# Maxima last in the transposed scores, and the query, key and transposed-score products next to each other

## What is computed

```
win    = windows of x, 64 tokens each               # (8*16, 64, 128)
normed = layernorm(win) * ln1_g + ln1_b
q,k,v  = split(normed @ in_w.T + in_b), 8 heads of 16
attn   = softmax(q @ k.T / 4)                       # 64 x 64 for each window and head
y      = win + (attn @ v) @ out_w.T + out_b
y      = y + silu(layernorm2(y) @ fc1_w.T + fc1_b) @ fc2_w.T + fc2_b
```

## Time and profile before

| | |
|---|---|
| median of three runs | 374.71 us (373.15 to 374.91) |
| profiled execution | 375.25 us, its span 373.4 us |
| PE matmul busy | 346.6 us, 93% |
| DVE, ACT, POOL busy | 293.6, 241.8, 167.2 us |
| one image in the loop | about 41.9 us: 23.0 us for the odd step (158.94 to 181.99) and 18.9 us for the even step (181.99 to 200.87), from scores 0 to scores 0 |
| granted TensorE clock | 0.986 of full speed on average |

### The profile page before, as it was taken

The page is one execution under the profiler, slowest core; times in us unless marked ns, Lnnn a source line. Parts: engine busy times, 40 slices in busy tenths (PEclk is TensorE's granted clock), DMA queues, the critical chain, the costliest instruction groups (busy, mean ns, idle before and its releaser), DMA issues.

```text
span 373.4 us, 9822 instructions
## 1 busy us (share of the span) xinstructions
PE 346.6 (93%) x3349; PEld 292.5 (78%) x3349; DVE 293.6 (79%) x862; ACT 241.8 (65%) x438; POOL 167.2 (45%) x176
## 2 busy tenths in 40 slices
PE   3678999999999999999999999999999999999764
PEld 2477788888888888888888888888888888878552
DVE  8478889798798878798798878798798878686552
ACT  1425678684968578684968578684969578665440
POOL 6353064636446434635456434635455434441420
PEclk9989999999999999999999999999999999999898
DMA  4132130302122121303122121303122120300001
GB/s 130 31 92 71 43 87 31 88 27 65 64 83 71 30 82 56 94 19 76 59 75 70 34 78 56 101 11 77 63 72 68 35 77 31 87 2 28 30 1 56
DMA packets 31715, 21.98 MB, mean 59 GB/s; under 512 B 22417, under 2 KB 23505, under 8 KB 31697
## 3 DMA queue, kind: packets, MB, share of 16 engines
q1 hardware_dynamic: 31696, 21.75, 21.3%
HBM read 4.95 MB, written 4.19 MB: 24 GB/s over the span
## 4 chain that ended last, share of the span: by engine, by line
PE 75%; DVE 6%; issue 5%; ACT 2%; POOL 1%; DVEq 0%; POOLq 0%; ACTq 0%
PE p_scoreT L635 12%; PE p_c L530 12%; PE p_score L612 9%; PE p_attn L650 9%; PE p_a L530 6%; PE p_scoreT L630 4%; PE p_a L594 4%; PE p_c L708 4%; PE p_d L530 3%; DVE xn_tok L1106 3%; PE p_c L679 2%; PE p_a L578 2%; PE p_a L568 2%; PE p_c L685 2%; PE p_c L666 1%
## 5 line engine op out<-in xcount | busy, mean ns | idle before, releaser
L912 ACT ACTIVATE probs<-p_scoreT 128x512 f32<-128x512 f32 x64 | 38.6, 603 | 34.6 <-PE p_scoreT L635 34.1
L466 POOL TENSOR_TENSOR hid_l<-hid,hid_h 128x512 fp32r<-128x512 f32 x30 | 40.4, 1365 | 43.0 <-ACT hid_h L946 41.2
L612 PE MATMUL p_score<-kd_h,qd_h 128*128 128x128 f32 (+1 forms) x512 | 54.7, 250 | 0.8 <-DVE row_max L1159 0.8
L612 PEld LDWEIGHTS p_score<-kd_h,qd_h 128*128 128x128 f32 (+1 forms) x512 | 50.4, 164 | 5.8 <-DVE row_max L1159 2.2
L650 PEld LDWEIGHTS p_attn<-vd,probs 128*64 128x64 f32 x1024 | 36.2, 139 | 22.2 <-issue 15.1
L471 POOL TENSOR_TENSOR y_l<-y,y_h 128x512 fp32r<-128x512 f32 (+1 forms) x17 | 20.6, 1210 | 70.3 <-ACT y_h L926 70.3
L1159 DVE TENSOR_REDUCE row_max<-p_score 128x8 f32<-128x512 f32 x64 | 43.9, 686 | 7.9 <-PE p_score L612 7.9
L650 PE MATMUL p_attn<-vd,probs 128*64 128x34 f32 x1024 | 45.6, 245 | 2.6 <-ACT probs L912 2.6
L635 PE MATMUL p_scoreT<-qd_h,kd_h 128*128 128x256 f32 x128 | 41.6, 325 | 0.0
L458 POOL TENSOR_SCALAR kd_l<-k_l,head_a 128x512 fp32r<-128x512 f32 x16 | 26.7, 1670 | 32.2 <-DVE k_l L1141 21.1
L450 POOL TENSOR_TENSOR rstd<-rstd,minus_half 128x4 f32<-128x4 f32 (+1 forms) x33 | 35.5, 1075 | 2.8
(11 more groups left out here) (182 smaller groups left out, 871.0 us busy)
## 6 DMA issues: line engine op xcount, KB each, us to landing
x_in<-in_x SPq DMA_DIRECT2D x16, 256.0 KB, 2.8
qd_h<-q_h SPq DMA_DIRECT2D x64, 64.0 KB, 2.0
qd_l<-q_l SPq DMA_DIRECT2D x64, 64.0 KB, 2.0
vd<-v_tok SPq DMA_DIRECT2D x64, 64.0 KB, 2.2
out<-out_sb SPq DMA_DIRECT2D x16, 256.0 KB, 2.1
fc_rows<-in_L_conv_fc_w SPq DMA_DIRECT2D x2, 128.0 KB, 2.5
in_w_rows<-in_L_conv_in_w SPq DMA_DIRECT2D x1, 192.0 KB, 2.7
out_w_rows<-in_L_conv_out_w SPq DMA_DIRECT2D x1, 64.0 KB, 2.5
```

The source lines that it names most:

```text
L466: pool.tensor_tensor(hid_l[:, t], hid[:, t], hid_h[:, t].bitcast(F32), ALU.subtract).then_inc(hid_low[t], 1)
L612: last = pe.matmul(p_score[0:rows, 2 * KEYS * j:2 * KEYS * (j + 1)], qd_h[:, h.par, j, 2 * KEYS * p:2 * KEYS * p + rows], kd_h[:, h.par, 2 ...
L912: act.activation(probs[:, p % 2], p_scoreT[:].rearrange("row (win j q) -> row win j q", win=2, j=QUADS), ACT.Exp, scale=SCORE_SCALE).then_ ...
```

## The change

Two things are changed. In `b_scoreT`, the six products come first and the four maxima products last; the wait for `max_wide_ready` stands between them, and for p = 0 three waits (for the spread queries and keys) are repeated ahead of the products. In the steps, PE does `c_kv` ahead of `a_q`, and `a_k` directly behind `a_q` and ahead of `b_scoreT(b, 1)`; before, `a_k` stood behind `b_score(b, 3)` and `d_kvT`. ACT's list moves its own `a_k` ahead of the exponential of p = 1 accordingly. DVE's, POOL's and SP's lists are unchanged.

```
             def b_scoreT(h, p):
 
-                pe.wait_ge(max_wide_ready[p], h.n())
                 if p == 0:
+                    pe.wait_ge(q_high_dma, h.n(times=16 * QUADS))
+                    pe.wait_ge(kd_high[0], h.n())
+                    pe.wait_ge(kd_high[1], h.n())
                     pe.wait_ge(q_low_dma, h.n(times=16 * QUADS))
...
                 dst = p_scoreT[:].rearrange("row (win j q) -> row win j q", win=2, j=QUADS)
-                for j in range(QUADS):
-                    pe.matmul(dst[:, :, j, :], max_wide[:, p % 2, 2 * j:2 * j + 2, :],
-                              neg_ident[:], start=j == 0, stop=False, skip_group_check=True)
                 for win in range(2):
                     window = 2 * p + win
                     for k, (kd, qd) in enumerate(((kd_h, qd_h), (kd_h, qd_l), (kd_l, qd_h))):
-                        last = pe.matmul(dst[:, win], kd[:, h.par, window], qd[:, h.par, :, KEYS * window:KEYS * (window + 1)],
-                                         start=False, stop=win == 1 and k == 2, skip_group_check=True)
+                        pe.matmul(dst[:, win], kd[:, h.par, window], qd[:, h.par, :, KEYS * window:KEYS * (window + 1)],
+                                  start=win == 0 and k == 0, stop=False, skip_group_check=True)
+                pe.wait_ge(max_wide_ready[p], h.n())
+                for j in range(QUADS):
+                    last = pe.matmul(dst[:, :, j, :], max_wide[:, p % 2, 2 * j:2 * j + 2, :],
+                                     neg_ident[:], start=False, stop=j == QUADS - 1, skip_group_check=True)
                 last.then_inc(scoreT_ready[p], 1)
...
                 b_attn(b, 0)
                 if with_c:
                     c_yT(c)
-                if with_a:
-                    a_q(a)
                 if with_tail:
                     c_kv(tail)
+                if with_a:
+                    a_q(a)
+                    a_k(a)
                 b_scoreT(b, 1)
                 b_score(b, 3)
                 if with_d:
                     d_kvT(loop, -1)
-                if with_a:
-                    a_k(a)
                 b_attn(b, 1)
...
                 if with_a:
                     a_q(a)
+                    a_k(a)
                 b_exp(b, 1)
                 if with_a:
-                    a_k(a)
                     a_k_block(a, 0)
```

More of the change, by code:

```diff
@@ L779, in step @@
                     c_yT(c)
+                if with_tail:
+                    c_kv(tail)
                 if with_a:
                     a_q(a)
-                if with_tail:
-                    c_kv(tail)
+                    a_k(a)
                 b_scoreT(b, 1)
```

## The result

The changed kernel takes 372.49 us in the median of ten runs (370.96 to 377.03), against 375.12 us (373.09 to 376.27) for the kernel before on the same chip: ratio 0.9924, with an interval of 0.9901 to 0.9946. The forecast was 373.2 us, range 371.0 to 376.0. So it is faster, by 0.8% where 0.4% was forecast. Three of the ten, near 377.0 us, ran at a lower granted clock (0.966 or 0.967 on average, the others 0.984 to 0.990), and the ratio leaves them out.

The account below looks back on a forecast made before the run. PE's list, busy 93% of the span, was taken as the bound. Odd steps -1.9, even steps +0.9, last odd step -0.35 and image 1's even-step wait -0.15 gave -1.5 us: 373.2 us against the median, range 371.0 to 376.0.

Parts of the forecast that it names:

- odd, scores 1 to projection with its bare load: PE at the start of odd steps: the wait for `max_wide` goes, 1.96 to 1.79 us, 0.17 gained.
- odd, `c_yT` to attention 1: PE in odd steps: key products beside the query products shorten this stretch from 5.33 to 5.07 us, 0.26 less.
- odd, p = 2 in front of `d_mT`: Odd steps, where `d_mT` follows the scores of p = 2: maxima last loses 0.04 us (0 to 0.08).
- odd, `d_final` late by DVE: Odd steps: `d_final` waits for DVE's second-block matrix, which may come late; 0.08 us lost, between 0 and 0.3.
- even, scores 1 to projection: PE in even steps: 1.74 to 1.79 us, 0.05 lost, about half hidden where attention 0 waits for ACT.
- even, attention 1 waits for the exponential: Even steps: attention 1 directly follows scores 3 and waits for ACT's exponential, 4.57 to 4.63 us, 0.06 lost.
- even, `xn_tok` later: DVE's statistics chain in even steps comes 0 to 0.70 us later, delaying PE's next odd step; 0.05 us taken.
- The price of 0.08: On PE, each full load of 128 fp32r columns behind a short bf16 product leaves 0.08 us not hidden.
- part 1 alone gives zero: Maxima last in `b_scoreT`: by the bare loads alone nothing is gained, one of 0.08 us leaves and one comes.
- the slower rival: Even steps, `row_max` of p = 3 to `xn_tok`: DVE's delay passed on whole, +4.6 us, to 377.8 us; chance 0.12.
- the whole gain arrives: Rival: no give-backs, odd steps -0.43 us, even steps 0, in all -3.1 us, to 371.6 us; chance 0.26.
- The bound does not move: Rival: odd steps' gain is spent waiting for ACT or DVE, -0.2 us a loop image or less, 374.3 us; chance 0.18.

Follow-up runs that it names:

- part1: Kernel before with the maxima products last in all four transposed scores, the old order of the steps kept: 374.63 us, ratio 0.9995.
- extra_full2: Changed kernel plus one unused DVE reduction of 0.68 us in every even step, ahead of the statistics: ratio 0.9990 to the kernel before.
- last01: Changed kernel with the maxima last only at p = 0 and 1, first again at p = 2 and 3: 371.59 us, ratio 0.9917 to the kernel before.
- aggregate2: Changed kernel with DVE aggregating the next half's statistics ahead of `yn_l` in even steps: ratio 0.9926 to the kernel before.
- norm_early: best2 with DVE doing `yn_tok` ahead of `row_max` of p = 3 in even steps: ratio 0.9948 to the kernel before.
- best2: aggregate2 with the maxima last only at p = 1 and, in odd steps, p = 0: ratio 0.9941 to the kernel before.

## Why the prediction was right, and where its sizes were off

The direction and the mechanism held, but the sum for an image of the loop was half of what came. The profile's span lost 2.9 us where -1.5 was forecast; the fourteen steps of the middle lost 2.07 where the sum has -1.9 + 0.9 - 0.15 = -1.15. The forecast's steps, before to after, in means over the loop:

| step of the forecast | forecast | measured |
|---|---|---|
| odd, scores 1 to projection with its bare load | 1.96 to 1.79 | 1.95 to 1.79 |
| odd, `c_yT` to attention 1 | 5.33 to 5.07 | 5.33 to 5.05 |
| odd, p = 2 in front of `d_mT` | +0.04 | +0.06 |
| odd, `d_final` late by DVE | +0.08 | 0.00 |
| odd, p = 3 | 0 | +0.01 |
| even, scores 1 to projection | +0.05, half hidden | +0.05, of which 0.02 comes back by `c_yT` |
| even, attention 1 waits for the exponential | 4.57 to 4.63 | 4.57 to 4.59 |
| even, `xn_tok` later | +0.05 | about +0.01 |
| even, p = 2 | 0 | -0.02 |
| even, p = 3 | 0 | +0.11 |
| odd, wait at `a_back` | 0 | -0.10 |

- **The price of 0.08 was right**, and so were both sums made from it. The projection's group grew from 0.70 to 0.78 and scores 3 in odd steps from 0.73 to 0.82. The first score product took 0.12 behind the key products and 0.17 behind the scores. The three repeated waits cost nothing that shows: scores 1 take the 0.74 of the sum. In the trace of the change a load of 128 fp32 columns takes 188 ns in the median (L634) and one of 128 bf16 columns 98 ns (L638). By the Trainium skill ("TensorE: Matmul & The Clock Gate", section "LDWEIGHTS (loading the stationary operand)") a load of 128 columns, at 107 ns, would leave some 0.05 bare (0.06 by its figure), an estimate; the trace doesn't agree, since the rows at the new places say 0.08 again and the fp32 loads last longer, so the measurement decides. That part 1 alone gives zero held: part1 changed an image by 0.01.
- **Mis-sized, `d_final`.** I took 0.08 a step in odd steps. The first `d_final` group stands at the same distances before and after (2.20 behind `d_mT`). DVE's matrix was not the last to arrive.
- **Mis-sized, the exponential.** Forecast +0.06, measured +0.02 to 0.03. The wait exists, 0.06 in the rows above, but the exponential starts 3.94 behind `c_yT`, where my sum had 3.71 + 0.22 + 0.05 = 3.98.
- **Mis-sized, and the larger error, the end of the even step.** I called the trade at p = 2 and 3 even except in front of `d_mT`. In the even step's p = 3 it isn't: behind the attention, whose loads have 64 columns, the first L634 now takes 0.22 (last rows of the even step above), and a second bare load stands behind the maxima in front of `fc1`. That is +0.11 (2.50 to 2.61), which the sum had left out. But it costs nothing: from the even step's transposition to `a_back` of the next step PE took 5.85 us before and 5.86 after. This stretch ends with PE's wait for `xn_tok`, so PE's 0.11 there only eats that wait (scores 0 to `a_back` 1.09 to 0.99). I had priced PE's wait as something that could only grow.
- **A term with no row in the forecast:** attention 1 in odd steps takes 0.61 instead of 0.64, 0.03 less. I name no cause.
- **One step where DVE's delay was passed on.** The sum put the steps of image 0 at about nothing. Its odd step lost 0.17: there the widening of p = 3 takes 0.80 us (in both kernels; 0.42 in even steps), so that DVE has less to absorb the delay with. In the changed kernel `yn_l` ends at 53.12 there and `fc1` starts at 53.26, 0.32 behind the maxima instead of 0.21. So the slower rival is real, but in one step of fourteen.

So odd steps gained 0.41 without the wait at `a_back`, against 0.31 forecast, and even steps with that wait lost 0.04, against 0.13: -0.37 an image in place of -0.18. The forecast erred by give-backs that it counted and that the slack absorbed. The rival "the whole gain arrives" (odd -0.43, even 0) lies nearer for the loop, and the device time of 372.49 lies between the two. That the device time came within 0.7 us of the forecast is in part luck: inside the steps of these means the gain was twice what the sum had, and outside them nearly all that it had was missing. For the odd step of image 0, the even step of image 1 and the last odd step the sum has 0, +0.13 - 0.15 and -0.35, together -0.37; the rows show +0.17, 0.00 and -0.20, together -0.03. "The bound does not move" and "DVE's delay is passed on" are excluded for the loop by its means, and extra_full2 shows that the second was not far away: 0.33 us an image. The price of the former doesn't follow from its own term: -0.2 an image for six images would be 373.5 us, not 374.3.

Of the 2.9 us between the two profiles 0.83 lie at the ends. The last odd step ran at a granted clock of 1.00 in both: from its scores 0 to its last L679 (now L682) PE took 20.21 us before and 20.01 after, so the step gave 0.20, where I had 0.35 for the wait that it lost. The other 0.63 lie where the clock differs: 0.25 at the start (0.95 and 1.00) and 0.38 behind that step (0.87 and 0.79). How much of these is the change and how much the clock stays open.

## What to carry to other kernels

In this kernel a short product left 0.08 us of the load behind it bare, and moving the short product moved the bare load and did not remove it. Put it where the engine behind is released by the last short product and nobody waits for the load, and put 512-column products next to those whose loads they can hide. Before pricing a small loss, ask which stretch between two waits it lies in: inside a stretch that another engine's chain sets, PE's losses and PE's gains both come out near zero, here 0.11 lost and 0.01 paid, and in last01 0.10 gained and 0.09 of it waited away. And when one wait is taken away, look at once for the next to arrive: aggregate2 and norm_early only exchanged waits.

## What the runs showed of the hardware

- What stays bare depends on the product in front. To the next product, the first L634 takes 0.12 behind a 512-column product, 0.17 behind the scores, whose last product has 64 stationary columns, and 0.22 behind the attention (64 stationary columns, 34 moving). Behind the maxima (128 moving columns in bf16) the first product takes 0.20.
- The cast that widens the maxima has a median of 0.46 us and takes up to 1.31 us for the same shape. At p = 0 its end follows POOL and not its own start: between 100 and 250 us of five kernels (before, the change, aggregate2, best2, norm_early) it ends 1.55 to 1.57 us behind the start of POOL's pair of `hid_l` (1.37 us each), whether it takes 0.53 or 1.13. The Trainium skill ("SBUF — State Buffer", on its two physically separate sides) calls the port pair that DVE and GpSimd share an exclusive lock, held for a whole instruction. That fits, and so do the even steps, where the cast takes 0.42 (195.23) and `kd_l` of POOL beside it 1.84, where it takes 1.57 in odd steps. What doesn't fit is the cast of 0.60 at 173.46, which ends while a `kd_l` from 173.10 on still runs; POOL's spans are rough, and no run here varied this.
- The loop's means repeat within 0.01 us between the two profiles of the changed kernel, while its device times spread by 6.2 us in twelve executions (last01's by 0.7 us in six). For effects under 0.5% here the trace's means are the better scale, and a ratio without them misleads: best2's loop is 0.56 us an image shorter than that of the kernel before and 0.19 shorter than the change's, and its ratio is about the change's (0.9941 and 0.9938).
